# Dot-product layers of a graph stack, reassociated: one weight product for the scores, rows of h as values, Wv at the output's turn

## The reference

```python
h = maximum(layernorm(x), 0)                      # before each layer
# L0: one head, no biases
Q, K, V = h @ W_q, h @ W_k, h @ W_v
out = softmax(where(adj == 0, -1e9, Q @ K.T / 8)) @ V
# L1: four heads, with biases
v, q, k = h @ Wv[i] + bv[i], h @ Wq[i] + bq[i], h @ Wk[i] + bk[i]
s = leaky_relu(q @ k.T / 8, 0.2) - 1e10 * (1 - adj)
out = leaky_relu(mean over i of softmax(s) @ v, 0.2)
```

## Time and profile before

| | before |
|---|---|
| median of 3 runs | 3647.93 us (3643.5 to 3651.93) |
| profiled execution | 3658.79 us, span 3656.9 us |
| busy over the span | PE 86%, DVE 86%, ACT 82%, POOL 27% |
| mean granted TensorE clock | 0.96 |

### The profile page before, as it was taken

How to read it: one execution, slowest core, us unless ns; L and a number is a source line. 1 busy time by engine, 2 the same in 40 slices (tenths; PEclk the granted TensorE clock), 3 DMA queues, 4 the chain that set the end, 5 groups by cost and what they waited for, 6 DMA issues and landing times. The chain is left out here.

```text
span 3656.9 us, 79212 instructions
## 1 busy us (share of the span) xinstructions
PE 3145.9 (86%) x31515; PEld 1741.2 (48%) x31515; DVE 3129.5 (86%) x4797; ACT 2982.5 (82%) x3625; POOL 1005.0 (27%) x565
## 2 busy tenths in 40 slices
PE   7996998999999869889898898988988989968885
PEld 5663666666666633333333333333333333336764
DVE  6665887888888779999999999999999999956666
ACT  5664887887788759999999999999999999956555
POOL 4432655655566610100000000000010000016554
PEclk9997999999999989999999999999999999988788
DMA  6540000000000000000000000000000000001111
GB/s 229 207 141 16 22 16 19 19 19 19 19 19 19 22 7 10 10 10 10 10 10 12 11 10 10 10 10 10 10 10 10 10 10 10 13 17 57 51 52 35
DMA packets 67251, 110.62 MB, mean 30 GB/s; under 512 B 25941, under 2 KB 25944, under 8 KB 66904
## 3 DMA queue, kind: packets, MB, share of 16 engines
q1 hardware_dynamic: 66904, 105.77, 9.3%
HBM read 86.87 MB, written 18.87 MB: 29 GB/s over the span
## 5 line engine op out<-in xcount | busy, mean ns | idle before, releaser
L980 ACT ACTIVATE l_scalar_ring<-l_w,l_r 128x1024 f32<-128x1024 f32 x1632 | 1712.9, 1141 | 34.8 <-DVE l_values L1026 25.7
L1094 DVE TENSOR_SCALAR l_vector_ring<-l_w_code,l_r_code 128x2048 f32<-128x2048 f32 x1232 | 1588.9, 1354 | 3.1 <-issue 0.2
L917 PE MATMUL scores<-l_scalar_ring,l_signs 128*32 128x512 f32 x6528 | 792.0, 604 | 91.2 <-ACT l_scalar_ring L980 90.9
L927 PE MATMUL scores<-l_vector_ring,l_signs_code 128*32 128x512 f16 x9856 | 670.9, 393 | 140.1 <-DVE l_vector_ring L1094 139.3
L242 ACT COPY probs_t<-turned 128x512 f32<-128x512 f32 x576 | 324.7, 587 | 422.5 <-PE turned L201 422.3
L433 POOL TENSOR_TENSOR l_masked<-l_relu,mask 128x1024 f32<-128x1024 f32 x256 | 546.2, 2134 | 438.0 <-ACT l_relu L585 397.1
L927 PEld LDWEIGHTS scores<-l_vector_ring,l_signs_code 128*32 128x32 bf16 x9856 | 243.1, 95 | 592.1 <-DVE l_vector_ring L1094 308.8
L212 PE MATMUL outT<-probs_t,l_values 128*64 128x128 f32 x6144 | 433.9, 284 | 88.3 <-ACT probs_t L242 40.3
L212 PEld LDWEIGHTS outT<-probs_t,l_values 128*64 128x64 f32 x6144 | 343.1, 140 | 234.2 <-DVE l_acc L667 104.4
L269 ACT ACTIVATE l_probs<-l_logits,negmax 128x1024 f32<-128x1024 f32 x384 | 443.7, 1155 | 6.6 <-DVE negmax L260 6.6
L201 PE MATMUL turned<-ident,l_probs 128*128 128x128 f32 x3072 | 436.6, 287 | 12.1 <-issue 7.3
(11 more groups left out here) (239 smaller groups left out, 3148.1 us busy)
## 6 DMA issues: line engine op xcount, KB each, us to landing
mask<-masks_kept SPq DMA_DIRECT2D x192, 256.0 KB, 2.6
l_adj<-adj SPq DMA_DIRECT2D x64, 512.0 KB, 5.6
masks_kept<-l_mask_ring SPq DMA_DIRECT2D x64, 256.0 KB, 4.2
x_res<-x SPq DMA_DIRECT2D x8, 256.0 KB, 5.1
out<-x_res SPq DMA_DIRECT2D x8, 256.0 KB, 2.8
l_w_both<-L_gnn_Wq SPq DMA_DIRECT2D x2, 64.0 KB
l_w_both<-L_gnn_Wk SPq DMA_DIRECT2D x2, 64.0 KB
l_w_both<-L_gnn_Wv SPq DMA_DIRECT2D x2, 64.0 KB
```

Of the source, the lines that this page charges most:

```text
L917: last = nc.tensor.matmul(s.scores[g * ROWS:(g + 1) * ROWS, buf, half, :], signs[:, window], scalar_ring[:, at % SCALAR_RING, g, halves[ha ...
L927: last = nc.tensor.matmul(s.scores[g * ROWS:(g + 1) * ROWS, buf, half, :], signs_code[:, par, g % 2, window], parts(vector_ring[:, at % VE ...
L980: last = nc.scalar.activation(scalar_ring[:, at % SCALAR_RING, g, :], w[:, par, :], ACT.Relu, bias=r[:, par, column:column + 1])
L1094: last = nc.vector.tensor_scalar(vector_ring[:, at % VECTOR_RING, g:g + 2, :], w_code[:, par, :, :], r_code[:, par, 0, column:column + 1], ...
```

## The change

Scores are computed as h (Wq Wk^T) h^T: the product of the score weights is made once per layer, only the keys' side is projected (per head h times the product), and the queries' side of the scores is h itself, split in high and low parts (`h2`, now for two graphs). The values are rows of h, copied once per graph from y by DVE (`take_values`); Wv is applied in `turn_out`, in the place of `add_halves`. K becomes 4 in L0 and 12 in L1 (two turns of y, in L1 two fills for a per-key term of the biases, two per head for keys). In L0 they lie in n = 0 to 3, in L1 in n = 1, 3, ..., 23. In L1 the per-key term travels in two spare rows of the keys' low part, against constant rows of `h1`; DMAs on SP's queue place them once per graph (`stage`). The reciprocal leaves `finish`: it is taken in its own unit, between `logit` and `copy_out`, and the drain moves to the head of each unit, ahead of the half copy. The preparation of the weights is rewritten. In L0 POOL's centre and square of the next norm move from n = 3 and 4 to n = 1 and 2.

```diff
-def turn_out(pe, s, sems, u, fills_done, to=None, buffers=1):
+def turn_out(pe, s, sems, u, fills_done, to=None, buffers=1, weights=None):
...
-    QK = 2 * H
-    PIECES = 2
-    WIDTH = s.N // PIECES
-    K = 2 + PIECES * QK + H
+    R = D + 1 if b_dram else D
+    KEYS = 4 if b_dram else 2
+    K = KEYS + 2 * H
...
+        def fills_at(n, project):
+            if not project:
+                return []
+            if leaky:
+                return [n // 2] if n % 2 and n // 2 < K else []
+            return [n] if n < K else []
...
-            for o in range(3):
-                for to in (w_in[0:D, o, :, :], w_both[0:D, o, :, :], w_both[D:P, o, :, :]):
+            for o in range(2):
+                sp.dma_start(w_in[0:D, o, :, :], w_dram[o].rearrange("h i o -> i h o")).then_inc(sems["weights_in"], 16)
...
+                def stage(b):
+                    sp.wait_ge(sems["fill_copied"], b * K + KEYS)
+                    par = b % 2
+                    sp.dma_start(h1[0:D, par, :], h2[0:D, par, :]).then_inc(sems["staged"], 16)
+                    for h in range(H):
+                        sp.dma_start(kl[D:D + 1, par, h, :], dh[h:h + 1, :]).then_inc(sems["staged"], 16)
+                        sp.dma_start(kl[D + 1:D + 2, par, h, :], dl[h:h + 1, :]).then_inc(sems["staged"], 16)
...
+                    if m == 1:
+                        stage(0)
+                    if i == 5 and b + 1 < B:
+                        stage(b + 1)
...
-                    if n == (2 if leaky else 3):
+                    if n == (2 if leaky else 1):
                         layer_norm_centre(g, s, sems, next_norm(s, b), b + 2)
...
-                lhs = q2[:, par, h, i * P:(i + 1) * P]
...
-                    nc.tensor.matmul(out, lhs, kh[:, par, h, cols], start=True, stop=False)
-                    last = nc.tensor.matmul(out, lhs, kl[:, par, h, cols], start=False, stop=True)
+                    nc.tensor.matmul(out, h2[:, par, rows], kh[:, par, h, cols], start=True, stop=False)
+                    last = nc.tensor.matmul(out, h1[:, par, rows], kl[:, par, h, cols], start=False, stop=True)
...
-                        turn_out(pe, s, sems, u - 1, 0, unit_out)
+                        turn_out(pe, s, sems, u - 1, 0, unit_out, weights=wv[:, (n - 1) % H, :])
...
                     if n == 0:
-                        pe.wait_ge(sems["fill_copied"], (b + 1) * K)
-                    probs_times_values(pe, s, sems, values[:, par, :, n % H, :], u)
+                        pe.wait_ge(sems["values_ready"], b + 1)
+                    probs_times_values(pe, s, sems, values[:, par, :, :], u)
...
+            def take_values(b, par):
+                v.wait_ge(sems["y_ready"], b + 1)
+                nc.vector.tensor_scalar(values[:, par, :, :], s.y[:, par, :, :], 0.0, None, ALU.max
+                                        ).then_inc(sems["values_ready"], 1)
...
+            def inverse_sum(n):
+                slot = n % 4
+                nc.vector.reciprocal(s.rinv[:, slot:slot + 1], s.rowsum[:, slot:slot + 1])
...
             def finish(b, n, u):
-                nc.vector.reciprocal(s.rinv[:, slot:slot + 1], s.rowsum[:, slot:slot + 1])
-                v.drain()
...
                 for n in range(U):
                     u = b * U + n
+                    v.drain()
                     if leaky:
                         copy_half(v, nc.vector.tensor_copy, s, sems, 0, u)
...
                         logit(b, (n + 2) % U, u + 2)
-                    fills = steps_fills(n, project)
+                    inverse_sum(n)
...
                     copy_out(v, s, sems, u)
-                    for k in fills:
+                    for k in fills_at(n, project):
                         take_fill(b + 1, 1 - par, k)
+                    if n == (6 if leaky else 4) and project:
+                        take_values(b + 1, 1 - par)
+                v.drain()
                 finish(b, U - 1, b * U + U - 1)
...
+            if leaky:
+                nc.vector.memset(kl[D:P, :, :, :], 0.0)
+                nc.vector.memset(h1[D:P, :, :], 0.0)
+                v.drain()
+                nc.vector.memset(h1[D:D + 2, :, :], UP * CONST)
```

More of the change, by code:

```diff
@@ L524, in graph @@
                         score(b + 1, 1 - par, n + 3 - U, u + 3)
-                    fills = steps_fills(n, project)
-                    for k in fills[:1]:
+                    for k in fills_at(n, project):
                         fill(b + 1, 1 - par, k)
@@ L529, in graph @@
                     if n == 0:
[L530 to L534 removed]
+                        pe.wait_ge(sems["values_ready"], b + 1)
+                    probs_times_values(pe, s, sems, values[:, par, :, :], u)
+                turn_out(pe, s, sems, b * U + U - 1, 0, unit_out, weights=wv[:, H - 1, :])
@@ new lines, in _ @@
+            if b_dram:
+                last = nc.tensor.matmul(bias_bank[0:H, H:H + 1], bias_prod[0:D, :], one[0:D, :], start=True, stop=True,
+                                        skip_group_check=True)
+            last.then_inc(sems["bound_ready"], 1)
+            pe.wait_ge(sems["weights_ready"], 3)
+            nc.tensor.matmul(bound_bank[:, 0:H * R], ones[0:R, :], wabs[0:R, :, :].rearrange("p h r -> p (h r)"), start=True,
+                             stop=True).then_inc(sems["bound_ready"], 1)
@@ L598, in graph @@
                         relu(n + 3, u + 3)
-                    for k in steps_fills(n, project):
+                    for k in fills_at(n, project):
                         high_part(b + 1, 1 - par, k)
@@ L713, in _ @@
+            last.then_inc(sems["weights_ready"], 1)
+            v.wait_ge(sems["bound_ready"], 2)
+            nc.vector.tensor_copy(product[0:R, :, :].rearrange("p h r -> p (h r)"), top_bank[0:R, 0:H * R])
+            v.drain()
+            nc.vector.scalar_tensor_tensor(out=wabs[0:R, :, :], in0=product[0:R, :, :], scalar=-1.0, in1=product[0:R, :, :],
+                                           op0=ALU.mult, op1=ALU.max).then_inc(sems["weights_ready"], 1)
             if adj_dram is not None:
@@ L747, in _ @@
+            for twice in range(2):
+                last = nc.vector.tensor_tensor(w_low[:, :, twice, :], w_scaled[:, :, 0:D], w_high[:, :, twice, :], ALU.subtract)
+            last.then_inc(sems["weights_ready"], 1)
             for k in range(K):
@@ L751, in _ @@
                     layer_norm_mean(v, s, sems, 1, 1)
-                if adj_dram is not None and k == 4:
+                if adj_dram is not None and k == 3:
                     layer_norm_scale(v, s, sems, 1, 1)
+            take_values(0, 0)
             logit(0, 0, 0)
```

235 lines of the change are left out of this document (120 added, 115 removed).

## The result

The kernel after takes 3600.03 us, median of 4 runs (3593.72 to 3616.46), beside 3645.72 for the kernel before (median of 4, 3640.03 to 3651.93): a ratio of 0.9882, 95% interval 0.9863 to 0.99. That is 46 us less by the two medians, 43 by the ratio, and 36 to 50 by the interval. Run again with 13 runs of before beside it: 0.9886 (0.9862 to 0.9911). The forecast was 3611. The profiled execution took 3603.63 us (span 3601.8) against 3658.79.

A forecast was written before the change was run, and what follows sets the result against it. No engine's total bounds L1; three loops between engines do, and a double fill costs L0. From 3658.8, -17 -4 -10 -8 gives 3620; the same gain from the 3647.9 median gives 3609, rounded up to 3611; range 3580 to 3636.

The forecast's parts named there:

- 1, L0's double fill: L0's unit 4: one fill each in units 0 to 3 cuts the 5.88 interval to about 3.5; -17 us.
- Rival C: L0 held by its loads of adjacency masks, so the double fill's gain vanishes: 3628 us; chance 0.10.
- 2, L0's start: Start of L0: fewer weight loads, bounds and fills, first fill at about 16 us; -4 us, ends 1 and 7.
- 3, L1's start: Start of L1: fewer fills and weight loads, less new clears, staging level with residuals; -10 us, ends 4 and 14.
- 4, the reciprocal: L1's plain units: moving it gains almost nothing, 3.33 stays about 3.33; 0.1 less every fourth unit.
- Rival D: L1: the reciprocal's move pays in full, 0.15 to 0.2 a unit, if POOL's mask starts earlier: 3568 us; chance 0.14.
- the mask's loop: L1's loop two, through POOL's mask, logits, output copy and PE: 9.94 us for three units, 3.31 each.
- 5, the drain: L1's drain ahead of the half copy: costs 0.15 after a fill, covered by DVE's idle time in plain units.
- Rival E: Slower: the drain is uncovered in every L1 unit, 0.23 us each with the reciprocal: 3670 us; chance 0.05.
- 6, fills: L1's twelve fills for 22: -0.3 to -0.6 per four units, +0.3 where values' fills were; -1.7 us a graph.
- 7, the values' copy: L1's unit n = 6, new DVE copy without cover: 0.5 us ahead of POOL's mask, 2.0 behind; 0.7 taken per graph.
- rival B: The port: all seven values' copies in L1 start behind POOL's mask, 2 us a graph with the slip: 3625 us; chance 0.12.

The follow-up runs named there:

- The experiment: Kernel after with both of L0's keys' fills put back in unit 4, the second behind the product: 3618.86 us, ratio 0.9924, L0's loop 13.4 us longer.
- the drain ahead of the logits: Kernel after with L1's reciprocal ahead of the logits and L1's drain moved from the unit's head to behind it: ratio 0.9889, L1's loop 963.3 us.
- three experiments: Kernel after with fills in n = 0 to 11 (0.986); with the values' copy at n = 7 (3628.66 us); with those fills, reciprocal before logits, copy at n = 18 (0.9891).
- Reciprocal put back: Kernel after with the reciprocal and its drain returned to `finish`: ratio 0.9898, L1's loop 958.5 us.
- the early reciprocal: Kernel after with L1's reciprocal ahead of the logits instead of behind them: 3594.76 us, ratio 0.987, L1's loop 949.9 us.
- the values' copy cut: Kernel after with the values' copy cut to one eighth in graphs 1 to 7 of both layers, values there wrong: 3593.99 us, L1's loop 953.7 us.

## Why the prediction held, point by point

**1, L0's double fill.** Right: -17.2 for -17. The experiment splits it into 13.4 and 3.8, so the interval of 5.88 against 3.51 was a good price by luck in part: the fill taken out of unit 4 gave 1.9 a graph and not 2.37, the other edits in L0 gave the rest. Rival C fell with it.

**2, L0's start.** Right: -4.6 for -4, the first fill at 15.65 for "about 16". That is 3.0 ahead of the first fill and 1.6 behind it, where the fewer fills alone were put at 3. The kernel's second profile has -5.3.

**3, L1's start.** Right: -9.6 for -10, of which 2.2 ahead of the first fill, 7.1 from there to the scores and 0.3 behind. From first fill to first scores 14.8 (14.4 forecast, 21.9 before), the first scores at 301.82 ("near 302"). The two rows were called level; staging is later: residuals of the keys end near 300.2, the last issue ends at 300.5, and the scores are released by that DMA. Nine issues take 0.63 from one to the next, not 0.5, and the scores start 1.3 behind the last issue's end, where the 1.5 to land had stood on no row. The clears took 6.14 for the estimate of 6.4: 4096 words 3.47, 2048 halves 1.76. The Trainium skill, "VectorE: DVE Perf Modes", section "Zero memsets can be issued as uint32 (trn2)", has a clear cost a cycle per element, whatever its type, and the trace agrees: 0.85 ns a word, 0.86 ns a half.

**4, the reciprocal.** Right in kind. A plain unit gained 0.10 (eighth graph, 109.1 to 106.0), where I gave 1 us to the eighth graph and it was 3. The same 3.1 came with the move alone, so it is the reciprocal's; step 4 had 3.34 to 3.36 for a unit of 3.33 and so no gain but the head mean's. Rival D fell: the move alone gave 5.2, with the mask's loop next, as argued.

**5, the drain.** 0.16 to 0.17 behind a keys' fill, as priced. "Covered in plain units" was too strong: where DVE comes late from the logits, its half copy starts 0.10 to 0.31 behind ACT's with no idle time of DVE left ahead of the drain. No run took the drain out of plain units alone, so its price there is open; with the reciprocal's gain they still came out 0.10 shorter. Rival E fell; the drain ahead of the logits shows that its cover is a matter of place.

**6, fills.** The sum was right, its terms were not. Per four units, fifth graph: n = 8 to 11 gave -0.58 (-0.5 forecast), n = 16 to 23 +0.78 (+0.6). But n = 0 to 7 and 12 to 15 gave -0.98 together where I had 1.6, n = 12 to 15 only -0.10: POOL's norm stands in that group (n = 12), and the loop over POOL doesn't shrink with fills. The pairs are 7.21, not 7.3, and what they gained by the reciprocal and the drain is 0.03 and not 0.2: the base is 7.24 for a keys' fill in every second unit, not 7.49.

**7, the values' copy.** Mis-sized: 0 for 0.7 a graph. I had written that it had no cover; 0.60 of DVE's idle time was behind it. The race with POOL was called rightly (0.39 ahead, forecast 0.3), and all sixteen copies took 0.40 to 0.42. So rival B didn't happen here, but its price is real in three experiments: 1.21, 1.08 and 2.33 where the copy started 1.20, 1.34 and 0.08 behind POOL's mask. In each it ends 0.28 behind the mask. The Trainium skill's rule from "SBUF — State Buffer", "Who interferes with whom", agrees: the later one waits out the other's whole instruction, and with the copy 0.03 ahead it is POOL that is longer, by 0.24. That section also says that a DVE instruction with two inputs in SBUF contends with POOL's reads; the head mean at 1.92 for 0.23 agrees.

In the fifth graph the errors of 6 (0.8 too much gain) and 7 (0.7 too much cost) cancel: -0.91 for a forecast of -1.0. Over all seven it is -3.8 (-7 forecast), or -8.6 without the long firsts, which no step had and which took back 4.8 (0.8 of the -8.6 are the two turns of the hardware loop); the eighth gave 2 more than forecast. So the prediction was right by good sums for the layers' starts and for L0, and partly by luck for L1.

**Long firsts.** In three graphs of the kernel after (the first, fourth and sixth; in its second profile the first, fourth and seventh) unit 0 takes 5.1 to 5.25. Table of windows, the fourth graph's first units, kernel after:

```profile
684.00:686.00 2.00, 2.00 (x24) 2.00 (x22) 0.30 (x3) 1.06 (x2) 1.46 (x1) 0.50 0.03 10
```

Reciprocal put back:

```profile
684.00:686.00 2.00, 2.00 (x27) 1.76 (x24) 1.09 (x3) 0.71 (x2) 1.96 (x1) 1.00 0.00 0
```

The granted clock is 0.50 here, that is the lower of TensorE's two levels (1.2 GHz), and 1.00 there. The same y fill shows it in the timeline, kernel after:

```profile
683.33 1.97 PE L505 MATMUL fill<-l_up,y 128*64 128x128 f32 x16
```

Reciprocal put back:

```profile
682.84 1.09 PE L505 MATMUL fill<-l_up,y 128*64 128x128 f32 x16
```

Ahead of it PE had idled 1.14, 0.50 and 1.76 in the kernel after, at the step from one graph to the next, where DVE takes the head mean and the norm's mean before it copies the output; 0.97, 0.53 and 1.72 with the reciprocal put back; but also 1.17, 0.56 and 1.70 with the early reciprocal, where the clock stayed at 1.00. So those idle times alone don't tell a long first from a short one. No run varied them by themselves, and what tips it stays open.

**The rest of the 46 us.** The layers touched give 38.3, 39 forecast. That the later layers moved was named as something that would make the forecast wrong; in the profiles they did, by 16.8, but these lie in unchanged code whose time spreads by 23 us over the profiles, with the clock granted in the last layer. The kernel after's second profile has 2335.4 there, 7.5 more than its first, and the kernel before with the reciprocal's move alone has 2328.6, as short as the kernel after's 2327.9. The medians' difference, 45.7, is between 38.3 and 55.2, and the interval (36 to 50) includes 38.3. Whether the change helps the last layer's clock at all was not settled.

## What to carry to other kernels

Price a step from an instruction of the very kind that stays: behind a queries' fill the next transposes came 0.26 later than behind a keys' fill, and a whole step was built on the wrong one. Look at what DVE waits for directly behind a new instruction before calling it uncovered, and in each kind of unit before calling it covered. A one-source SBUF copy on DVE beside a busy POOL is free or costs two microseconds depending on who starts first by a tenth; keep it where DVE is ahead by its whole length, and when something else on DVE moves, look at it again.

## What the runs showed of the hardware

- A DVE copy of 128x512 from SBUF to SBUF (0.42 alone) that started 0.08, 1.20 or 1.34 behind POOL's mask of 2.13 ended 0.28 behind the mask's end, in each of seven graphs. One that started 0.03 ahead kept its 0.42, and the mask took 2.37. A delay of DVE by 0.7 brought a second collision of 1.7.
- A drain between two DVE operations costs 0.16 to 0.17 from start to start ahead of a half copy; ahead of the logits the gap from half copy to logits grew by 0.39.
- PE's granted clock fell from the higher to the lower level behind some steps between graphs, at 1.6 us each: in 3 of 8 graphs in the kernel after (one of them right behind L1's start), in one with the values' copy cut, in none with the early reciprocal. At the two turns of L1's hardware loop it fell in every profile.
- The same last layer took 334.3 to 357.4 us over 14 profiles, at a mean granted clock of 0.90 to 0.82, the longer the lower.
